# Cross-attention and gated FFN on one core: another order of the opening, and 24 idle products on TensorE

## The chip, the core and the metric

The kernel runs on one core of a Trainium2 chip. Its engines are PE (TensorE, matrix products into PSUM), DVE (VectorE), ACT (ScalarE), POOL (GpSimd) and SP (SyncE, which here only issues transfers); ACT and POOL issue some too. They run side by side and wait for each other by semaphores. The metric is the device time of one execution in microseconds (us), lower is better.

## What is computed

```python
x = x + attention(layernorm(x), ctx, ctx, pos, mask, Wq, Wk, Wv, Wo)   # rotary positions on q and k
x = x + ffn(layernorm(x), weight, bias, gate_w, in_scale, out_scale)
# x, ctx: (32, 64, 512) float32; 32 query heads, 8 key/value heads of 128
# ffn: routing = softmax(xf @ gate_w.T); (xf * (routing @ in_scale)) @ sign(weight).T * (routing @ out_scale) + bias
```

## The kernel before

The 2048 rows of x make 16 tiles of 128 rows, worked in four quarters of four tiles (512 rows). Every quarter has eight slots, one for each key/value group; slot U projects its group (K, four query heads Q1 to Q4, V), does the attention of the group before it and the output product of the group before that. So slot 0 has projections only, slot 1 projections and attention, and slot 2 is the first with output products. Slots also prepare the tiles of the next quarter (context, table rows, normalised x) and do the FFN of the quarter before; the last quarter's FFN stands at the end.

A product is kept exact to about float32 by three products of a split form: hi·hi, hi·lo, lo·hi. A projection is therefore 12 instructions on PE (four pieces of the contraction, three products each, lines 1045 to 1047) into one PSUM bank of 128x512. Each 128x512 weight tile is loaded to one of five ring buffers `raw` (SP, `load_weights`), copied by ACT to its upper half (`split_hi`, line 511), and POOL subtracts to get the lower half (`split_lo`, line 408). Three pairs of buffers hold the halves of projection weights, `w_hi` and `w_lo`; four hold those of the output weights (wo). A load waits for the split five loads before it. After a K or Q projection DVE rotates the result by the position tables (`rotate`, lines 801 and 803) and POOL adds the two parts (`rope_sum`, line 415).

The opening, ahead of slot 0, is `first_quarter` on each engine: positions go to DVE and from it to POOL, which gathers four tiles of the rotary table (line 382); four context tiles are transposed by PE (line 1034), split by ACT (hi) and DVE (lo, line 736); x's four tiles get statistics on DVE, the root on POOL (`s_rstd`, line 397), the normalisation on DVE (line 1002), and are transposed and split likewise. Then come the transposes of the table rows, whose copies on ACT are cosT and sinT. `ffn_constants` prepares the FFN: signs of its weight (DVE, lines 1015 and 1017) and their transposes, the gate's transpose, the scales. Each engine runs its instructions in the order in which they are written, so the order of the source is the schedule. STREAM is the order in which a slot's ten weight tiles (0 K, 1 to 4 Q, 5 V, 6 to 9 wo) are loaded and split.

## Time and profile before

| | us |
|---|---|
| median of 3 runs | 1192.29 |
| lowest and highest | 1191.25, 1193.23 |
| the profiled execution | 1192.27 |
| its span from first to last instruction | 1189.5 |
| PE busy | 1156.4 (97%) |
| DVE busy | 809.9 (68%) |
| POOL busy | 712.0 (60%) |
| ACT busy | 552.3 (46%) |

Busy time is the sum over an engine's instructions. A row of a timeline gives start, duration and instruction; what stands in brackets is the idle time of the engine before it and what ended that. Consecutive instructions of PE overlap, so their step (start to start) is shorter than their duration.

### The profile page before, as it was taken

How to read it: one execution, taken by the hardware profiler on the slowest of the kernel's cores; microseconds unless marked ns; L12 is line 12 of the kernel's file. 1: busy time of each engine (PE TensorE's matmuls, PEld its weight loads, DVE VectorE, ACT ScalarE, POOL GpSimd, SP SyncE). 2: the span in 40 equal slices, each digit the busy share in tenths (PEclk: the TensorE clock that was granted, in tenths of full speed). 3: DMA queues.
4: the chain of work that ended last, by engine and by line, in shares of the span. 5: the costliest groups of instructions: out<-in, count | busy, mean ns of one | idle time of the engine just before them, and what ended most of it. 6: DMA issues, size and time to landing. Idle time of an engine off the chain costs nothing.

```text
span 1189.5 us, 23750 instructions
## 1 busy us (share of the span) xinstructions
PE 1156.4 (97%) x7636; PEld 949.7 (80%) x7636; DVE 809.9 (68%) x1367; ACT 552.3 (46%) x1768; POOL 712.0 (60%) x593
## 2 busy tenths in 40 slices
PE   5699999999999999999999999999999999999997
PEld 4588888888888888888888888888888888888875
DVE  6767676667776766777766667667677666666764
ACT  3444445444543544444544544544544444535442
POOL 5666655555775656765555766655667555766525
PEclk9999999999999999999999999999999999999997
DMA  8234333223422322333322322323332222322200
GB/s 227 79 111 120 93 94 89 79 81 100 121 90 63 88 79 88 120 99 97 107 67 71 106 79 87 97 83 105 89 98 81 64 72 68 97 75 87 78 2 35
DMA packets 136923, 106.02 MB, mean 89 GB/s; under 512 B 12776, under 2 KB 111080, under 8 KB 136864
## 3 DMA queue, kind: packets, MB, share of 16 engines
q1 hardware_dynamic: 131488, 94.78, 27.5%
q10 hardware_dynamic: 4608, 8.39, 2.1%
q0 software_dynamic: 768, 2.10, 0.6%
q8 instruction: 33, 0.54, 0.2%
q14 instruction: 26, 0.21, 0.1%
HBM read 101.05 MB, written 4.19 MB: 88 GB/s over the span
## 4 chain that ended last, share of the span: by engine, by line
PE 94%; DVE 3%; POOL 1%; issue 1%; ACT 1%; DMA 0%; POOLq 0%; DVEq 0%; ACTq 0%
PE chunk L1045 25%; PE chunk L1046 24%; PE chunk L1047 24%; PE o_ps L1118 5%; PE sc_ps L1093 3%; PE tr_ps L1093 2%; PE aux L1034 2%; PE o_ps L1034 1%; PE tr_ps L1034 1%; PE sc_ps L1034 1%; PE aux L1195 1%; PE aux L1196 1%; PE aux L1169 1%; PE aux L1181 0%; ACT probs L547 0%
## 5 line engine op out<-in xcount | busy, mean ns | idle before, releaser
L408 POOL TENSOR_TENSOR w_lo<-raw,w_hi 128x512 fp32r<-128x512 f32 x192 | 247.0, 1298 | 384.6 <-ACT w_hi L511 384.4
L801 DVE TENSOR_TENSOR swp<-chunk,sinT 64x512 f32<-64x512 f32 x320 | 220.3, 689 | 98.8 <-PE chunk L1047 94.4
L1045 PE MATMUL chunk<-xT_hi,w_hi 128*128 128x512 f32 (+1 forms) x512 | 210.0, 410 | 2.0 <-POOL w_lo L408 1.8
L1046 PE MATMUL chunk<-xT_lo,w_hi 128*128 128x512 f32 (+1 forms) x512 | 201.6, 394 | 0.0
L1047 PE MATMUL chunk<-xT_hi,w_lo 128*128 128x512 f32 (+1 forms) x512 | 200.6, 392 | 0.0
L1045 PE MATMUL chunk<-wo_hi,oT_hi 128*128 128x512 f32 x496 | 196.7, 397 | 0.1
L1047 PE MATMUL chunk<-wo_hi,oT_lo 128*128 128x512 f32 x496 | 193.7, 391 | 0.0
L1046 PE MATMUL chunk<-wo_lo,oT_hi 128*128 128x512 f32 x496 | 193.2, 389 | 0.0
L415 POOL TENSOR_TENSOR qT<-qT,swp 128x512 f32<-128x512 f32 x128 | 166.1, 1298 | 41.2 <-DVE qT L803 39.2
L547 ACT ACTIVATE probs<-scores,neg_max 128x64 f32<-128x64 f32 x512 | 170.4, 335 | 28.5 <-DVE neg_max L758 28.5
L743 DVE TENSOR_TENSOR acc<-chunk,acc 128x512 f32 (+1 forms) x128 | 88.2, 689 | 139.3 <-PE chunk L1047 139.1
L408 POOL TENSOR_TENSOR wo_lo<-raw,wo_hi 128x512 fp32r<-128x512 f32 x128 | 165.1, 1302 | 0.0
L511 ACT ACTIVATE w_hi<-raw 128x512 fp32r<-128x512 f32 x192 | 117.7, 629 | 61.2 <-issue 45.9
L1045 PEld LDWEIGHTS chunk<-xT_hi,w_hi 128*128 128x128 f32 x512 | 97.2, 190 | 25.3 <-DVE qT L803 2.2
L1047 PEld LDWEIGHTS chunk<-xT_hi,w_lo 128*128 128x128 f32 x512 | 96.6, 189 | 21.8
L1046 PEld LDWEIGHTS chunk<-xT_lo,w_hi 128*128 128x128 f32 x512 | 96.8, 189 | 17.4
L1045 PEld LDWEIGHTS chunk<-wo_hi,oT_hi 128*128 128x128 f32 x496 | 93.1, 188 | 20.8 <-issue 0.5
L1047 PEld LDWEIGHTS chunk<-wo_hi,oT_lo 128*128 128x128 f32 x496 | 93.1, 188 | 20.2
L1046 PEld LDWEIGHTS chunk<-wo_lo,oT_hi 128*128 128x128 f32 x496 | 93.2, 188 | 18.0
L1045 PE MATMUL chunk<-cT_hi,w_hi 128*128 128x512 f32 (+1 forms) x256 | 99.9, 390 | 1.3 <-DVE qT L803 1.3
L511 ACT ACTIVATE oT_hi<-o_ps 128x512 fp32r<-128x512 f32 x128 | 69.5, 597 | 66.4 <-PE o_ps L1118 66.4
L1047 PE MATMUL chunk<-cT_hi,w_lo 128*128 128x512 f32 (+1 forms) x256 | 99.9, 390 | 0.0
(281 smaller groups left out, 1934.7 us busy)
## 6 DMA issues: line engine op xcount, KB each, us to landing
raw<-in_L_xattn_Wo SPq DMA_DIRECT2D x132, 256.0 KB, 2.6
raw<-in_L_xattn_Wq SPq DMA_DIRECT2D x128, 256.0 KB, 2.7
raw<-in_L_xattn_Wk SPq DMA_DIRECT2D x32, 256.0 KB
raw<-in_L_xattn_Wv SPq DMA_DIRECT2D x32, 256.0 KB
acc<-in_x ACTq DMA_DIRECT2D x16, 256.0 KB, 2.9
c_tile<-in_ctx SPq DMA_DIRECT2D x12, 256.0 KB, 3.1
x_tile<-in_x SPq DMA_DIRECT2D x12, 256.0 KB, 3.4
result<-y ACTq DMA_DIRECT2D x12, 256.0 KB, 2.1
```

The source lines that it names most:

```text
L408: nc.gpsimd.tensor_tensor(lo, raw[:, n % RING, :], hi.bitcast(F32), ALU.subtract).then_inc(wsplit_lo, 1)
L415: nc.gpsimd.tensor_tensor(dst, dst, by_batch(swp[:, j % 2, :]), ALU.add).then_inc(roped, 1)
L511: return nc.scalar.activation(dst, src, ACT.Copy)
L547: last = nc.scalar.activation(probs[:, d, bass.ts(k, S)], scores[:, 2 * d + k // 4, bass.ts(k % 4, S)], ACT.Exp, bias=neg_max[:, d, k:k + ...
L743: nc.vector.tensor_tensor(a, chunk[OUT_BANK[p]][:, :], a, ALU.add).then_inc(added, 1)
L801: last = nc.vector.tensor_tensor(swp[to, k, :], bank[of, :], sinT[to, here], ALU.mult)
L1034: return nc.tensor.transpose(dst, src, ident[:, :])
L1045: nc.tensor.matmul(bank, a_hi, b_hi, start=i == 0, stop=False)
L1046: nc.tensor.matmul(bank, a_hi, b_lo, start=False, stop=False)
L1047: last = nc.tensor.matmul(bank, a_lo, b_hi, start=False, stop=i == n - 1)
L1093: last = nc.tensor.matmul(DUO_BANK[d][a * S:(a + 1) * S, bass.ts(place, S)], qT[:, hp, queries], kT[:, bass.ts(at, S)], start=True, stop=True)
L1118: last = nc.tensor.matmul(o_both[:, b, bass.ts(i, HG * S)], v[keys, 2 * d + i, :], probs_of[keys, i, :], start=k == 0, stop=k == 2)
```

## The change

The opening is written in another order, and what belongs to it moves:

- SP no longer issues the positions; ACT does, as its first transfer, then context tiles 2 and 3 and x tiles 2 and 3. SP issues context 0 and 1, K's weight, x tiles 0 and 1, and V's, Q1's, Q2's and Q3's weights, Q4's when a buffer is free, and only then the constants.
- Slot 0 loads six weight tiles in the order K, V, Q1 to Q4 (`FIRST_STREAM`); its four wo loads and splits, of a group that slot 0 does not have, are gone. All later ring numbers shift by it.
- PE does K's projection between context's and x's transposes, and V's ahead of Q's. PE gets 8, 12 and 4 products of the identity with itself in three places of `first_quarter`, into a bank nobody reads before it is written again.
- POOL clears its four buffers ahead of the gathers, and splits K and V ahead of the root of x and Q1 behind it; in slot 0 it alternates split and sum, and it splits the next slot's first two tiles there.
- The signs of the FFN weight are taken by ACT in place in slot 0 (`ACT.Sign`), no longer by DVE in two instructions a tile. PE's constants come behind all of slot 0's projections.
- Slot 1 has an order of its own on PE, DVE and ACT (`first_attention`): K's projection ahead of the scores, three projections between the scores and the transposes of the probabilities, and two weight splits between the exponentials of the two halves.

PE in the opening, from the last context tile (o_ps<-ident,qT) on: x_tile, f_tile, fT and y are the four normalised x tiles, scores holds the table rows, cT is the transposed context. Before:

```order
L1034 MATMUL o_ps<-ident,qT 128x128 x4
L1034 MATMUL chunk<-ident,x_tile 128x128 x4
L1034 MATMUL chunk<-ident,f_tile 128x128 x4
L1034 MATMUL o_ps<-ident,fT 128x128 x4
L1034 MATMUL aux<-ident,y 128x128 x4
L1034 MATMUL sc_ps<-ident,scores 128x128 x4
L1034 MATMUL tr_ps<-ident,scores 128x128 x4
L1045 MATMUL chunk<-cT_hi,w_hi 128x512
```

And in the change:

```order
L1122 MATMUL o_ps<-ident,qT 128x128 x4
L1393 MATMUL chunk<-ident 128x128 x12
L1133 MATMUL chunk<-cT_hi,w_hi 128x512
...
L1393 MATMUL chunk<-ident 128x128 x4
L1122 MATMUL chunk<-ident,x_tile 128x128 x4
L1122 MATMUL o_ps<-ident,f_tile 128x128 x4
L1122 MATMUL sc_ps<-ident,fT 128x128 x4
L1122 MATMUL aux<-ident,y 128x128 x4
L1122 MATMUL tr_ps<-ident,scores 128x128 x4
L1122 MATMUL o_ps<-ident,scores 128x128 x4
```

K's projection has moved from behind the table rows to ahead of x, between two groups of idle products.

POOL from its constants to the first sums (w_lo is a split, kT and qT are sums). Before:

```order
L388 MEMSET half 128x4
L382 DMA scores<-rope_table,pos_first 128x256 x4
L393 MEMSET c_tile 128x512
L393 MEMSET vT 128x512
L393 MEMSET probs 128x512
L393 MEMSET route 128x128
L397 TENSOR_TENSOR s_rstd<-s_var,half 128x4
L408 TENSOR_TENSOR w_lo<-raw,w_hi 128x512 x4
L408 TENSOR_TENSOR wo_lo<-raw,wo_hi 128x512
L461 MEMSET scores 128x1024
L415 TENSOR_TENSOR kT<-kT,swp 128x512
```

And in the change:

```order
L409 MEMSET half 128x4
L411 MEMSET c_tile 128x512
L411 MEMSET probs 128x512 x2
L411 MEMSET route 128x128
L403 DMA scores<-rope_table,pos_first 128x256 x4
L422 TENSOR_TENSOR w_lo<-raw,w_hi 128x512 x2
L536 TENSOR_TENSOR s_rstd<-s_var,half 128x4
L422 TENSOR_TENSOR w_lo<-raw,w_hi 128x512
L539 MEMSET scores 128x1024
L422 TENSOR_TENSOR w_lo<-raw,w_hi 128x512
L429 TENSOR_TENSOR kT<-kT,swp 128x512
```

The memsets went ahead of the gathers, two splits went ahead of s_rstd, and the wo split is gone.

ACT in slot 1, from V's rows (v_hi) to the values' first half (oT_hi). Before:

```order
L511 ACTIVATE v_hi<-o_ps 128x512
L511 ACTIVATE w_hi<-raw 128x512
L547 ACTIVATE probs,ssum<-scores,neg_max 128x64 x16
L511 ACTIVATE pT_hi<-sc_ps 128x512
L511 ACTIVATE w_hi<-raw 128x512
L511 ACTIVATE wo_hi<-raw 128x512
L511 ACTIVATE pT_hi<-tr_ps 128x512
L511 ACTIVATE oT_hi<-o_ps 128x2x4x64 x2
```

And in the change:

```order
L548 ACTIVATE v_hi<-o_ps 128x512
L548 ACTIVATE w_hi<-raw 128x512
L584 ACTIVATE probs,ssum<-scores,neg_max 128x64 x8
L548 ACTIVATE wo_hi<-raw 128x512
L548 ACTIVATE w_hi<-raw 128x512
L584 ACTIVATE probs,ssum<-scores,neg_max 128x64 x8
L548 ACTIVATE wo_hi<-raw 128x512
L548 ACTIVATE w_hi<-raw 128x512
L548 ACTIVATE pT_hi<-sc_ps 128x512
L548 ACTIVATE pT_hi<-tr_ps 128x512
L548 ACTIVATE oT_hi<-o_ps 128x2x4x64 x2
```

The 16 exponentials are cut in two halves with two splits between them, and two splits moved ahead of the probabilities' first copy.

The diff, cut to its core:

```diff
+    FIRST_STREAM = [0, PROJ - 1, 1, 2, 3, 4]
+        def ring_use(s, n):
+            return (n % RING, n // RING + 1) if s.first_proj else ((n - HG) % RING, 2 * s.U + (n - HG) // RING + 1)
+        def split_count(s, n):
+            return n + 1 if s.first_proj else s.U * CH - HG + n + 1
...
+                    if s.first_proj and n == 0:
+                        for p in range(2):
+                            sp.dma_start(acc[:, p, :], row_of(x_t, p)).then_inc(x_first_in[p], 16)
+                if s.first_proj:
+                    load_constants()
...
 # POOL
+            def first_projections(s):
+                second = Slot(0, 1, False, False)
+                for n in range(3, PROJ):
+                    split_lo(s, n)
+                    rope_sum(s, n - 3)
+                split_lo(second, 0)
+                rope_sum(s, KQ - 2)
+                split_lo(second, 1)
+                rope_sum(s, KQ - 1)
...
+            def first_quarter():
+                wait_alone(pool, pos_first_ok, 1)
+                for p in range(PAIRS):
+                    gather_rows(rows_first[:, p, :], pos_first[:, p:p + 1]).then_inc(rows_first_in, 16)
+                split_lo(first, 0)
+                split_lo(first, 1)
+                pool.wait_ge(x_st3, PAIRS)
+                nc.gpsimd.tensor_tensor(s_rstd[:, :], s_var[:, :], half[:, :], ALU.pow).then_inc(x_st4, PAIRS)
+                split_lo(first, 2)
+                wait_alone(pool, rows_tr, PAIRS)
+                nc.gpsimd.memset(scores[:, :, :], MASKED).then_inc(fill_ok, 1)
...
 # ACT
+            def first_projections(s):
+                split_hi(s, 3)
+                v_out(s)
+                split_hi(s, 4)
+                act.wait_ge(fw_in, 16)
+                for c in range(EC):
+                    nc.scalar.activation(fw[:, c, :], fw[:, c, :], ACT.Sign).then_inc(fw_sgn, 1)
+                split_hi(s, 5)
+                act.wait_ge(sc_in, 16 * 6)
...
 # PE
+            def first_projections(s):
+                for j in (5, 1, 2, 3, 4):
+                    project(s, j)
+                ffn_constants()
+            def first_attention(s):
+                project(s, 0)
+                pe.wait_ge(gate_ok, 1)
+                pe.wait_ge(fw_ok, EC)
+                v_rows(s)
+                scores_of(s, 0)
+                scores_of(s, 1)
+                project(s, 1)
+                project(s, 2)
+                project(s, 3)
+                probs_T(s, 0)
+                probs_T(s, 1)
+                project(s, 4)
+                values(s, 0)
+                project(s, 5)
+                pe.wait_ge(sc_lo, 2)
+                values(s, 1)
...
+            def idle_products(count):
+                for n in range(count):
+                    nc.tensor.matmul(chunk[0][:, bass.ts(n % EC, P)], ident[:, :], ident[:, :], start=True, stop=True)
...
                 pe.wait_ge(ident_ok, 2)
+                idle_products(8)
                 for p in range(PAIRS):
                     pe.wait_ge(c_first_in[p], 16)
                     transpose_tile(C_BANK[p], c_first[:, p, :]).then_inc(c_tr, 1)
+                idle_products(12)
+                project(Slot(0, 0, False, False), 0)
+                idle_products(4)
                 for p in range(PAIRS):
                     pe.wait_ge(xn_ok, p + 1)
                     transpose_tile(X_BANK[p], x_first[p]).then_inc(x_tr, 1)
...
 # DVE
+            def first_attention(s):
+                v_lo_split(s)
+                soft_a(s, 0)
+                soft_a(s, 1)
+                rotate(s, 0)
+                rotate(s, 1)
+                soft_b(s, 0)
+                soft_b(s, 1)
+                rotate(s, 2)
+                pT_lo_split(s, 0)
+                rotate(s, 3)
+                pT_lo_split(s, 1)
+                out_lo(s, 0)
+                out_lo(s, 1)
+                rotate(s, 4)
+                out_lo(s, 2)
+                out_lo(s, 3)
```

## Rows read from the trace of the kernel before

**Rows 1.** Stretches: us, busy PE, PEld, DVE, ACT, POOL (instructions), clock, DMA share, GB/s.

```profile
0.00:75.29 75.29, 52.52 (x304) 42.14 (x305) 53.16 (x82) 30.83 (x80) 46.22 (x47) 0.98 0.53 146
75.29:1160.00 1084.71, 1083.27 (x7243) 890.05 (x7242) 743.76 (x1258) 513.48 (x1667) 650.20 (x534) 1.00 0.29 87
1160.00:1189.50 29.50, 20.65 (x92) 17.47 (x90) 12.96 (x28) 7.94 (x22) 15.59 (x13) 0.75 0.09 36
```

**Rows 2.** PE's waits up to 75 us: us in total, times, longest.

```profile
PE aux L1034 <- DMA qT<-in_ctx: 7.9, 1, 7.9
PE chunk L1034 <- DVE x_tile L1002: 5.4, 1, 5.4
PE tr_ps L1034 <- DVE probs L768: 2.0, 1, 2.0
PE chunk L1045 <- POOL w_lo L408: 1.8, 1, 1.8
PE sc_ps L1034 <- DVE probs L768: 1.7, 1, 1.7
```

**Rows 3.** Timeline of PE: start us, us, instructions; in brackets idle before and releaser.

```profile
17.30 1.11 PE L1034 MATMUL chunk<-ident,x_tile 128*128 128x128 f32 x4 [5.42 <-DVE x_tile L1002]
...
19.91 1.06 PE L1034 MATMUL aux<-ident,y 128*128 128x128 f32 x4
20.77 0.67 PE L1034 MATMUL sc_ps<-ident,scores 128*128 128x128 f32 x4
...
21.63 0.47 PE L1045 MATMUL chunk<-cT_hi,w_hi 128*128 128x512 f32 x1
...
24.48 0.39 PE L1045 MATMUL chunk<-xT_hi,w_hi 128*128 128x512 f32 x1
...
75.29 0.39 PE L1045 MATMUL chunk<-wo_hi,oT_hi 128*128 128x512 f32 x1
```

**Rows 4.** Busy time by stretch, around the low clock in slot 1.

```profile
58.40:62.00 3.60, 3.60 (x10) 2.66 (x9) 1.51 (x3) 0.00 (x0) 2.68 (x3) 0.53 0.53 145
```

**Rows 5.** Timeline of POOL.

```profile
10.88 0.95 POOL L382 DMA_INDIRECT scores<-rope_table,pos_first  x1 [0.30 <-issue]
...
14.67 1.06 POOL L397 TENSOR_TENSOR s_rstd<-s_var,half 128x4 f32<-128x4 f32 x1 [1.23 <-DVE s_var L999]
15.71 1.25 POOL L408 TENSOR_TENSOR w_lo<-raw,w_hi 128x512 fp32r<-128x512 f32 x1
...
38.24 1.75 POOL L408 TENSOR_TENSOR wo_lo<-raw,wo_hi 128x512 fp32r<-128x512 f32 x1
```

**Rows 6.** Timeline of DVE.

```profile
5.15 0.18 DVE L978 CAST pos_f<-pos_i 128x16 f32<-128x16 int32 x1 [5.15 <-DMA pos_i<-in_pos_BxS]
...
15.76 1.49 DVE L1002 TENSOR_SCALAR x_tile<-acc,s_mv,s_rstd 128x512 f32<-128x512 f32 x1 [1.27 <-POOL s_rstd L397]
17.17 0.54 DVE L1002 TENSOR_SCALAR f_tile<-acc,s_mv,s_rstd 128x512 f32<-128x512 f32 x1
...
22.25 1.55 DVE L1015 TENSOR_SCALAR probs<-acc 128x512 f32<-128x512 f32 x1
...
30.64 0.69 DVE L1017 SCALAR_TENSOR_TENSOR acc<-acc,probs 128x512 f32<-128x512 f32 x1
```

**Rows 7.** Timeline of PE, the router's logits in a loop slot.

```profile
364.44 0.96 PE L1169 MATMUL aux<-gateT,fT 128*128 128x8 f32 x8
```

**Rows 8.** Busy time by stretch, early transfers.

```profile
5.00:10.00 5.00, 2.02 (x9) 1.66 (x10) 1.72 (x6) 0.60 (x1) 2.47 (x3) 1.00 1.01 352
```

**Rows 9.** The page's groups: busy us, mean ns, idle before and releaser.

```profile
L408 POOL TENSOR_TENSOR w_lo<-raw,w_hi 128x512 fp32r<-128x512 f32 x192 | 247.0, 1298 | 384.6 <-ACT w_hi L511 384.4
L801 DVE TENSOR_TENSOR swp<-chunk,sinT 64x512 f32<-64x512 f32 x320 | 220.3, 689 | 98.8 <-PE chunk L1047 94.4
...
L415 POOL TENSOR_TENSOR qT<-qT,swp 128x512 f32<-128x512 f32 x128 | 166.1, 1298 | 41.2 <-DVE qT L803 39.2
```

**Rows 10.** Groups by form up to 75.29 us.

```profile
L547 ACT ACTIVATE probs<-scores,neg_max 128x64 f32<-128x64 f32 x16 | 5.3, 334 | 2.4 <-DVE neg_max L758 2.4
```

More of the change, by code:

```diff
@@ L270, in jobs_of, with loads_of, rank, proj_bank @@
             return t, f, tile_in(s, i) if s.residual else None
+        def loads_of(s):
+            return FIRST_STREAM if s.first_proj else STREAM if s.proj else [PROJ + h for h in range(HG)]
+        def ring_use(s, n):
+            return (n % RING, n // RING + 1) if s.first_proj else ((n - HG) % RING, 2 * s.U + (n - HG) // RING + 1)
+        def split_count(s, n):
+            return n + 1 if s.first_proj else s.U * CH - HG + n + 1
+        def rank(s, j):
+            return FIRST_STREAM.index(j) if s.first_proj else j
+        def proj_bank(s, j):
+            return chunk[0 if s.first_proj and j == PROJ - 1 else PROJ_BANK[j]]
         def one(tile):
@@ L320, in load_weights @@
             def load_weights(s):
-                for n in range(CH):
-                    if s.first_proj and n == RING:
-                        load_constants()
-                    c, r = STREAM[n], n % RING
+                for n, c in enumerate(loads_of(s)):
+                    r, _ = ring_use(s, n)
                     if c >= PROJ:
@@ L451, in slot @@
                 if s.proj:
-                    for n in range(3):
+                    for n in range(2 if s.first_attn else 0, 3):
                         split_lo(s, n)
@@ L458, in slot @@
                     split_lo(s, 4)
-                if s.first_proj:
-                    wait_alone(pool, rows_tr, PAIRS)
-                    nc.gpsimd.memset(scores[:, :, :], MASKED).then_inc(fill_ok, 1)
-                if s.proj:
                     rope_sum(s, 0)
@@ L516, in split_hi @@
             def split_hi(s, n):
-                c = STREAM[n] if s.proj else PROJ + n
-                r = n % RING
-                act.wait_ge(raw_in[r], 16 * ((CH // RING) * s.U + n // RING + 1))
+                c, (r, use) = loads_of(s)[n], ring_use(s, n)
+                act.wait_ge(raw_in[r], 16 * use)
                 if c < PROJ:
-                    if not (s.first_proj and c < WRING):
-                        act.wait_ge(proj_done, s.U * PROJ + c - WRING + 1)
-                    hi = flat(w_hi[:, c % WRING, :, :])
+                    k = rank(s, c)
+                    if not (s.first_proj and k < WRING):
+                        act.wait_ge(proj_done, s.U * PROJ + k - WRING + 1)
+                    hi = flat(w_hi[:, k % WRING, :, :])
                 elif s.proj:
@@ L633, in attend_last @@
                 pT_hi_split(s, 1)
+            def first_attention(s):
+                ffn_constants()
+                split_hi(s, 2)
+                v_in_rows(s)
+                split_hi(s, 3)
+                exp_duo(s, 0)
+                split_hi(s, 4)
+                split_hi(s, 5)
+                exp_duo(s, 1)
+                split_hi(s, 6)
+                split_hi(s, 7)
+                pT_hi_split(s, 0)
+                pT_hi_split(s, 1)
+                out_hi(s, 0)
+                out_hi(s, 1)
+                split_hi(s, 8)
+                split_hi(s, 9)
+                v_out(s)
+                out_hi(s, 2)
+                out_hi(s, 3)
+            def first_projections(s):
+                split_hi(s, 3)
+                v_out(s)
+                split_hi(s, 4)
+                act.wait_ge(fw_in, 16)
+                for c in range(EC):
+                    nc.scalar.activation(fw[:, c, :], fw[:, c, :], ACT.Sign).then_inc(fw_sgn, 1)
+                split_hi(s, 5)
+                act.wait_ge(sc_in, 16 * 6)
+                copy(in_sc[:, :], in_raw[:, :]).then_inc(sc_hi, 1)
+                copy(out_sc[:, :], out_raw[:, :]).then_inc(sc_hi, 1)
+                second = Slot(0, 1, False, False)
+                split_hi(second, 0)
+                split_hi(second, 1)
             def slot(s):
@@ L638, in slot @@
                     return attend_last(s)
-                if s.proj and not s.first_proj:
+                if s.first_proj:
+                    return first_projections(s)
+                if s.first_attn:
+                    return first_attention(s)
+                if s.proj:
                     split_hi(s, 0)
```

151 lines of the change are left out of this document (72 added, 79 removed).

## The prediction

> **What bounds the kernel now.** I read three views, the stretches first. The busy time by stretch [rows 1] shows where PE is short of work in the span of 1189.5 us: from 75.29 us, when slot 2 begins with the first output product, until 1160 us PE is busy 1083.27 of 1084.71 us, while the opening has 52.52 busy of 75.29 us. So the middle costs what PE's instructions cost, and an edit of the opening is worth exactly what it moves slot 2's start, if nothing new waits afterwards. The waits of PE before 75 us [rows 2] name the losses: 7.9 us for the first context tile, 5.4 us for the normalised x, then 1 to 2 us each for softmax, a weight split and a rotation. The timeline [rows 3] gives the marks: x transposes from 17.30, the first projection (K) at 21.63, the second at 24.48, slot 2 at 75.29.
>
> A projection is 12 products, 2.85 us for the first (21.63 to 24.48), 0.228 a step and 2.73 in all where they follow each other.
>
> **TensorE's clock.** Four transposes step in 0.85 us at 19.91 and in 0.50 at 20.77 [rows 3], which are the two levels of 1.2 and 2.4 GHz, although the clock column says 1.00 there; the engine had done transposes without a gap since 17.30. From 58.4 to 62.0 us the column says 0.53 [rows 4], after PE had stood for 1.7 and 2.0 us [rows 2]: half the rate for 3.4 us, a loss of 1.7. The Trainium skill, page "TensorE: Matmul & The Clock Gate", section "Part 4: PE-mode transpose", says that transposes do not engage the full clock as they do not count as busy. The trace disagrees: nothing but transposes stood between 17.30 and the step up. By the page only the idle products and K's could raise the clock, and if those came too late the first rival below would be the result, 1181.0 us; by the row the clock is up before K and the sum stands.
>
> **Part 1, until x is transposed.** Times are those of before, re-chained.
> POOL: the four gathers end at 10.88 + 0.95 = 11.83 [rows 5]. They hang on the positions, which reach DVE at 5.15 [rows 6] after an issue at 0.8 from SP; now ACT issues them first at the same moment, so I keep 11.83. The four memsets (1.9 us there) move ahead of the gathers, into time in which POOL stood: nothing. Behind the gathers stand now two splits (K, V), 1.25 each [rows 5], ending at 13.1 and 14.35, and then s_rstd, 1.06 [rows 5], until 15.5. Before, it ended at 15.73. So K ahead of x costs x nothing: s_rstd is late by its place in POOL's order, but no later than it was.
> DVE: the first norm takes 1.49 instead of 0.54 [rows 6] beside POOL's split, and will again, as a split follows s_rstd as before. x tiles are ready at 17.0, 17.5, 17.95, 18.4 (steps of 0.46).
> PE: K's products wait for K's lower half, 13.1, and run to 15.9 at the full level. The four idle products, then x's transposes at 17.05, paced by the norms, end at 18.9; eight transposes of table rows, 1.0 us (20.77 to 21.63 before, at the full level but for the first), end at 19.9. V starts at 19.95. Before, K started at 21.63 [rows 3]. **Gain: 1.7 plus K's 2.7, 4.4 us.**
> Idle products: their price is not in the trace. Logits (four f32 products, two records each) take 0.96 us [rows 7] at the full level, so 0.24 a product for 8 columns, which I take; a product of 128 columns might cost twice that. At the low level it is 0.43 (records step as transposes do) to 0.85. The first 8 stand from 1.6 us while the context is on its way: over at 5.0 to 8.4, nothing, since context is wanted only by 13.1. The 12 end by 11.5 to 13.6: nothing to 0.5. The upper end with both at the low level (8.4, 11.9, then 12 x 0.43) is 17 and costs x some 2.4 us. The last 4 (1.0) end at 16.9, before 17.05. Without a reason for a gain in themselves, I book them at nothing and their effect as the clock.
> DMA: from 5 to 10 us the queues move 352 GB/s [rows 8]. Ahead of the last x tile stand 2.25 MB (context, x, K) and up to 1.25 MB that shares the engines (V, two Q, gathers): it lands between 10 and 13.6. It has to be there by 13.1 (statistics 1.3 us, s_rstd's turn at 14.35): nothing, at worst 0.5 us.
>
> **Part 2, from 19.95 to slot 2.** PE's own work: 11 projections 30.0, constants 5 x 0.44 = 2.2, V's rows 0.5, scores 2.0, probabilities 0.9, values 1.8: 37.4 us, thus 57.4 at the soonest. Before, 12 projections and the same 7.4 took 53.7 (21.63 to 75.29), so 13.5 us were waits and low clock. What waits now, from durations of 1.30 a split and a sum, 3 x 0.69 = 2.1 a rotation [rows 9], 2.65 for eight exponentials (8 x 0.33 [rows 10]):
> The signs leave DVE, where they stood for 9.1 us (22.25 to 31.33 [rows 6]) ahead of the first rotation; ACT makes them in 4 x 0.5 us after 24, when it has nothing else. K is rotated 21.2 to 23.4, Q1 (done 25.6) to 27.8. POOL alternates split and sum: split 3 until 23.0, 4 until 26.0, 5 until 30.4. Q3 may start at 26.0 and does at 28.3; Q4 may at 30.4 and starts at 31.0. No wo load is split here now: 4 x 1.3 us less on POOL in slot 0, which it does behind. Last rotation 36.0, last sum 37.4. PE does constants and the next K in 33.8 to 38.8, V's rows to 39.3 and scores at once: PE's waits there, for a split (1.8 [rows 2]), a rotation and a sum, go.
> Slot 1: softmax's first maximum 41.8, exponentials to 44.5 and 48.2 (a split and two between), rotations 43.2 to 47.5, normalised 48.3 and 49.2. PE runs three projections meanwhile, 41.3 to 49.6: the transposes of both halves wait for nothing, where they waited 1.7 and 2.0. Q4 50.5, values 53.2, V 54.2 (third rotation 54.1: level), values 57.1 to 58.0. The output product waits for the last wo split: out_hi ends at 55.8, ACT 0.5, two splits of 1.25, 58.8. Here about 1 us is left; with small gaps in the five level places I take 2.0 in all, bounds 0.3 and 5. **Slot 2 starts at 59.4, 15.9 us sooner.** Work behind it (rotation 4, sum, wo splits) ends by 60.3, and scores there are wanted at 62.
>
> **Part 3, the loops and the end.** The same instructions in the same order, with ring numbers shifted by one and the same distance between load and split: nothing. In the last stretch the clock averages 0.75 [rows 1]; where its low part falls can shift by a few products: 1.7 us either way.
>
> **Sum.** The profiled execution took 1192.27 us, 2.8 over its span, and lies at the median of the three runs, 1192.29. 1192.3 - 4.4 - (13.5 - 2.0) = 1176.4.
>
> **Rivals.**
> Low clock in the opening: the idle products do not raise it, and K, x's and the rows' transposes go at half. For: they did until 20.77. Against: 12 idle products and K's twelve follow each other. K 13.2 to 18.3, products 20, transposes 23.5, rows 24.6: 4.6 us, 1181.0. Chance 0.08.
> POOL sets the pace: from 19.95 it has a memset and 22 pieces, 28.7 us at 1.30, against 37.4 of PE; beside DVE's two-input work pieces of 1.75 occur [rows 5], and all level places depend on it. Late weights work alike. Price 3, 1179.4. Chance 0.14.
> Softmax still waits: the splits put between ACT's exponentials hold them, and 3.7 us of waits with 1.7 of low clock stay. 5.4 us, 1181.8. Chance 0.07.
> Idle products too long, as priced above: 2.4 us, 1178.8. Chance 0.05.
> Better than the walk: no wait left and a luckier end, 1173.5. Chance 0.06.
> Little comes of it: x or its transposes come 4 us later by DMA and all 11.5 us of waits stay; 1192. Chance 0.01.
> Slower: the shifted ring makes a split late in every loop slot. In the loops PE waits for a split that POOL makes from a buffer whose load waits for the split five earlier; if that came short by a piece, 1.3 us a slot, 31 slots, 40 us: 1216. It decides from 0.5 us a slot. Against: 1.4 us idle in the whole middle [rows 1] and an unchanged distance. Chance 0.03.
>
> **How the numbers follow.** The forecast, 1174 to 1179, has 0.56. Adding POOL's and the products' cases and most of the two at 1181 to 1182 gives 1173.5 to 1181.5 for eight in ten. A measurement can tell 0.2%, 2.4 us, from no change: faster 0.95, same 0.02, slower 0.03.
>
> **What would show it.** In the profile after: V's products at 19 to 21 us, K's ended before x's transposes; s_rstd ending at 15 to 16; x's transposes stepping 0.44 a tile, not 0.87; no DVE signs; PE waits before slot 2 under 6 us behind 20 us, none over 1.5; a clock of 1.00 from 13 us to the last stretch; the first output product at 58 to 61. I am wrong if s_rstd or a weight comes later than 17, if PE stands over 2 us between projections, or if the middle has new idle.

## Result and the profile after

The changed kernel takes 1177.47 us (four runs, 1177.19 to 1177.51), the kernel before 1191.89 in the runs beside it (1191.25 to 1193.23): a ratio of 0.9877, 95% interval 0.9860 to 0.9894, or 14.4 us less. The forecast was 1176.4 us, with a range of 1173.5 to 1181.5. The profiled execution took 1177.43 us, its span 1175.6. One execution each of e5_slot1_generic, e8_root_first and e10_both and one of the kernel before took 250 to 1100 us longer than the others of its kernel and is left out of every figure below, though the 1176.68 in the expectation of e10_both still counts one.

The first view of the kernel after is the busy time by stretch, as in [rows 1] (us, busy PE, PEld, DVE, ACT, POOL with instructions, clock, DMA share, GB/s). The stretches are the opening up to slot 2, the loops, the end.

```profile
0.00:60.62 60.62, 54.67 (x352) 45.93 (x353) 44.15 (x70) 31.17 (x81) 41.70 (x42) 1.00 0.60 163
60.62:1145.00 1084.38, 1082.63 (x7238) 889.60 (x7239) 745.00 (x1260) 513.05 (x1666) 649.95 (x534) 1.00 0.29 87
1145.00:1175.60 30.60, 21.76 (x95) 18.34 (x94) 13.61 (x30) 8.10 (x22) 15.65 (x14) 0.76 0.09 35
```

The opening shrank from 75.29 to 60.62 us, and the middle is as full as before. PE's busy time in the opening rose by 2.15 us (7.67 us are idle products; the other work took 5.5 us less, a good part of which had been at the low level before); what fell is its standing time, from 22.77 to 5.95 us.

PE's waits up to slot 2 (us in total, times, longest), to be read against [rows 2]:

```profile
PE chunk L1393 <- POOL ident L407: 1.6, 1, 1.6
PE tr_ps L1122 <- DMA qT<-in_ctx: 1.5, 1, 1.5
PE chunk L1133 <- POOL w_lo L422: 1.4, 2, 0.8
PE chunk L1133 <- POOL wo_lo L422: 0.8, 1, 0.8
...
PE tr_ps L1122 <- DVE probs L843: 0.2, 1, 0.2
```

The 7.9 us for context and the 5.4 us for x are gone from the list, softmax's 2.0 and 1.7 are 0.2. No single wait is over 1.6.

PE's timeline (start us, us, instructions; in brackets the idle time before and its releaser), which answers [rows 3]. L1393 are the idle products, L1122 transposes, L1133 the first product of a step of a projection, L1206 the attention's values:

```profile
1.55 3.78 PE L1393 MATMUL chunk<-ident 128*128 128x128 f32 x16 [1.55 <-POOL ident L407]
...
9.93 2.84 PE L1393 MATMUL chunk<-ident 128*128 128x128 f32 x24
13.58 0.47 PE L1133 MATMUL chunk<-cT_hi,w_hi 128*128 128x512 f32 x1 [0.80 <-POOL w_lo L422]
...
16.42 1.05 PE L1393 MATMUL chunk<-ident 128*128 128x128 f32 x8
17.54 0.65 PE L1122 MATMUL chunk<-ident,x_tile 128*128 128x128 f32 x4
18.03 0.62 PE L1122 MATMUL o_ps<-ident,f_tile 128*128 128x128 f32 x4
...
20.20 0.48 PE L1133 MATMUL chunk<-cT_hi,w_hi 128*128 128x512 f32 x1
20.51 0.40 PE L1134 MATMUL chunk<-cT_lo,w_hi 128*128 128x512 f32 x1
...
50.56 0.66 PE L1122 MATMUL tr_ps<-ident,probs 128*128 128x128 f32 x4 [0.23 <-DVE probs L843]
51.78 0.47 PE L1133 MATMUL chunk<-xT_hi,w_hi 128*128 128x512 f32 x1 [0.56 <-POOL w_lo L422]
...
58.83 0.39 PE L1206 MATMUL o_ps<-pT_hi,v_hi 64*128 64x256 f32 x2 [0.16 <-DVE oT_lo L811]
...
60.62 0.49 PE L1133 MATMUL chunk<-wo_hi,oT_hi 128*128 128x512 f32 x1 [0.83 <-POOL wo_lo L422]
```

K's projection stands at 13.58, ahead of x's transposes (17.54); V's starts at 20.20, and slot 2 at 60.62, 14.67 us sooner than at 75.29. x's transposes step by 0.46 to 0.49, not 0.87: the clock is at 2.4 GHz by then.

POOL's timeline answers [rows 5]:

```profile
11.18 0.95 POOL L403 DMA_INDIRECT scores<-rope_table,pos_first  x1 [0.30 <-issue]
12.14 2.53 POOL L422 TENSOR_TENSOR w_lo<-raw,w_hi 128x512 fp32r<-128x512 f32 x2
14.89 1.06 POOL L536 TENSOR_TENSOR s_rstd<-s_var,half 128x4 f32<-128x4 f32 x1 [0.21 <-DVE s_var L1099]
15.93 1.27 POOL L422 TENSOR_TENSOR w_lo<-raw,w_hi 128x512 fp32r<-128x512 f32 x1
...
57.95 2.52 POOL L422 TENSOR_TENSOR wo_lo<-raw,wo_hi 128x512 fp32r<-128x512 f32 x2 [1.12 <-ACT wo_hi L548]
```

s_rstd comes behind two splits and still ends at 15.95, against 15.73 before. The last fence's final row is the wait of 0.83 in PE's list: POOL itself had waited 1.12 us for ScalarE's high part of the out_proj weights.

**Where the 13.9 us of span went.** Up to V's first product: K was started at 21.63 and took 2.85 there, V now starts at 20.20, so 1.43 + 2.85 = 4.28 us. From there to slot 2: 75.29 - 24.48 = 50.81 before, 60.62 - 20.20 = 40.42 now, 10.39 us. Behind slot 2: 1189.5 - 75.29 = 1114.21 before, 1114.98 now, 0.77 us the other way. 4.28 + 10.39 - 0.77 = 13.9.

### The profile page after: what moved, and what is told of

It reads as the page before. It is cut to its first block, busy times and chain, and to the rows that moved or that the text cites. A ratio compares the mean times of both kernels' runs of the same rounds, so it can differ in the third digit from the quotient of the medians.

```text
span 1175.6 us, 23824 instructions
## 1 busy us (share of the span) xinstructions
PE 1159.1 (99%) x7684; PEld 953.9 (81%) x7684; DVE 802.8 (68%) x1359; ACT 552.3 (47%) x1768; POOL 707.3 (60%) x589
## 4 chain that ended last, share of the span: by engine, by line
PE 95%; DVE 1%; POOL 1%; ACT 1%; issue 1%; DMA 1%; POOLq 0%; ACTq 0%; DVEq 0%
PE chunk L1133 25%; PE chunk L1134 24%; PE chunk L1135 24%; PE o_ps L1206 5%; PE sc_ps L1181 3%; PE tr_ps L1181 2%; PE aux L1122 2%; PE o_ps L1122 2%; PE tr_ps L1122 1%; PE sc_ps L1122 1%; PE aux L1286 1%; PE aux L1287 1%; PE aux L1260 1%; DMA qT<-in_ctx 1%; PE aux L1272 0%
## 5 line engine op out<-in xcount | busy, mean ns | idle before, releaser
L1133 PE MATMUL chunk<-xT_hi,w_hi 128*128 128x512 f32 (+1 forms) x512 | 208.9, 408 | 0.6 <-POOL w_lo L422 0.6
L1133 PE MATMUL chunk<-wo_hi,oT_hi 128*128 128x512 f32 x496 | 196.8, 397 | 1.2 <-POOL wo_lo L422 0.8
L422 POOL TENSOR_TENSOR wo_lo<-raw,wo_hi 128x512 fp32r<-128x512 f32 x124 | 159.3, 1297 | 4.8 <-ACT wo_hi L548 4.8
L1133 PEld LDWEIGHTS chunk<-xT_hi,w_hi 128*128 128x128 f32 x512 | 96.9, 189 | 23.2 <-issue 0.8
L1133 PEld LDWEIGHTS chunk<-wo_hi,oT_hi 128*128 128x128 f32 x496 | 93.1, 188 | 22.1 <-issue 1.8
L1133 PE MATMUL chunk<-cT_hi,w_hi 128*128 128x512 f32 (+1 forms) x256 | 100.0, 391 | 0.8 <-POOL w_lo L422 0.8
L1134 PE MATMUL chunk<-cT_lo,w_hi 128*128 128x512 f32 (+1 forms) x256 | 99.8, 390 | 0.0
```

Source lines behind the costliest of these rows:

```text
L422: nc.gpsimd.tensor_tensor(lo, raw[:, r, :], hi.bitcast(F32), ALU.subtract).then_inc(wsplit_lo, 1)
L1133: nc.tensor.matmul(bank, a_hi, b_hi, start=i == 0, stop=False)
L1134: nc.tensor.matmul(bank, a_hi, b_lo, start=False, stop=False)
```

## The experiments

All marks come from one profiled execution of each kernel (us): K's, x's transposes', V's and slot 2's first instruction on PE, the distance from V to slot 2, the span behind slot 2, and that execution's time. "Times" are the lowest and highest of the kernel's runs. The runs came in several batches, in which the kernel before had medians of 1191.7 to 1192.3 us.

| kernel | K | x | V | slot 2 | V to slot 2 | rest | run | times |
|---|---|---|---|---|---|---|---|---|
| after | 13.58 | 17.54 | 20.20 | 60.62 | 40.42 | 1114.98 | 1177.43 | 1177.19 to 1177.51 |
| e12_after_again | 13.47 | 17.43 | 20.09 | 60.50 | 40.41 | 1114.90 | 1177.25 | 1177.12 to 1177.82 |
| e1_no_idle | 13.65 | 18.91 | 21.66 | 62.05 | 40.39 | 1115.15 | 1178.99 | 1177.19 to 1179.27 |
| e2_no_idle12 | 13.67 | 17.94 | 20.48 | 60.88 | 40.40 | 1114.42 | 1177.82 | 1177.82 to 1178.95 |
| e3_k_behind_x | 20.35 | 17.69 | 23.19 | 63.44 | 40.25 | 1115.56 | 1180.83 | 1179.99 to 1181.71 |
| e4_signs_dve | 14.38 | 18.11 | 20.65 | 67.23 | 46.58 | 1114.97 | 1184.01 | 1181.66 to 1184.01 |
| e5_slot1_generic | 13.95 | 17.68 | 20.23 | 67.44 | 47.21 | 1113.86 | 1183.17 | 1183.17 to 1184.77 |
| e6_exps_together | 14.12 | 17.84 | 20.38 | 64.72 | 44.34 | 1115.78 | 1182.35 | 1180.84 to 1182.59 |
| e8_root_first | 14.37 | 17.23 | 19.77 | 60.15 | 40.38 | 1114.55 | 1176.49 | 1175.98 to 1176.87 |
| e9_wo_early | 14.38 | 18.11 | 20.65 | 60.15 | 39.50 | 1114.95 | 1176.90 | 1176.39 to 1177.88 |
| e10_both | 13.78 | 16.60 | 19.14 | 58.62 | 39.48 | 1114.88 | 1175.29 | 1174.90 to 1175.57 |
| e11_consts_early | 14.13 | 17.87 | 20.41 | 60.76 | 40.35 | 1114.54 | 1177.12 | 1176.45 to 1178.00 |

The loops are the same in all of them, and their "rest" lies between 1113.86 and 1115.78. So an effect of under about 1 us has to be read from the marks, and from V to slot 2 above all, since V's own place also moves with the clock in the opening (below); the last column by itself does not settle it. The eight runs of the changed kernel in the first two rows have a median of 1177.39, which the differences below are taken against.

### The ruler: the changed kernel again

> The changed kernel itself once more, unedited, beside the three others on the same chip, as the ruler for differences of under 1 us: 1177.4 us, 0.3 either way. Where the opening's low clock falls otherwise than in its first profile (idle products or K's products at half the level), V's first product comes up to 0.8 us from 20.20 and the time moves with it.

1177.30 us (1177.12 to 1177.82), ratio 0.9879 (0.9862 to 0.9895). V came 0.11 us sooner and slot 2 0.12 sooner than in the first profile: the marks repeat to about 0.1 us.

### Without the idle products

```
-                idle_products(8)
...
-                idle_products(12)
...
-                idle_products(4)
```

> The change without its 24 idle products; all else as it stands. Theory of order (the gain is the moved work, the products only lift PE's clock a little sooner): K's projection begins at the low clock and is raised on its way, x's transposes start 1 to 1.5 us later than 17.5, V's products 0.7 to 3 us later than 20.2, so 1178 to 1180.5 us, likeliest 1179. Theory of the clock (the products carry a large part): the clock stays low until 20 us or more and the time rises by 4.6 us or more, over 1182.

1178.68 us (0.9887, 0.9870 to 0.9903), 1.3 us more. PE's timeline of e1_no_idle, K and what follows:

```profile
13.65 0.77 PE L1133 MATMUL chunk<-cT_hi,w_hi 128*128 128x512 f32 x1 [2.85 <-POOL w_lo L422]
14.21 0.63 PE L1134 MATMUL chunk<-cT_lo,w_hi 128*128 128x512 f32 x1
...
18.48 0.63 PE L1135 MATMUL chunk<-cT_hi,w_lo 128*128 128x512 f32 x1
18.91 0.81 PE L1122 MATMUL chunk<-ident,x_tile 128*128 128x128 f32 x4
19.56 0.60 PE L1122 MATMUL o_ps<-ident,f_tile 128*128 128x128 f32 x4
```

K starts at the same place but its products step by 0.43 instead of 0.23, the 1.2 GHz level, for all twelve; it holds x's transposes until 18.91, and V comes 1.46 us later. The level rises with x's transposes, so nothing behind them is slower. That is what the idle products buy: the level of K's projection, 1.3 us of the 14.4. One of the four runs, at 1177.19 us, was no slower than the changed kernel; it has no trace. The new order alone keeps 1191.7 - 1178.7 = 13.0, against the kernel before in the runs beside it.

With the first eight kept and only the twelve and the four out:

> Only the first 8 idle products stay, the 12 ahead of K and the 4 behind it are out. If the clock, once up at 7.3 us, outlives PE's idle time up to K's products (some 3.7 us with one product group missing), K and x are unchanged and the time is 1177.4 within 0.3 (the last 4 even stood in x's way by at most 0.2). If it falls there, K's 12 products or x's transposes go at half rate and it is 1178.5 to 1180.

1178.31 us (0.9889, 0.9872 to 0.9905), 0.9 us more. Here K's first seven products ran at the low level (steps of 0.43 until 16.79) and the others at the full one, so V came 0.28 us later than in the first profile; the profiled execution was the fastest of the four. The stretch at the low level in e2_no_idle12:

```profile
10.00:16.80 6.80, 3.38 (x10) 2.49 (x9) 5.42 (x11) 1.86 (x3) 6.24 (x6) 0.50 1.05 286
```

PE's wait of 3.42 us for K's split began only at 10.25, so it is not the wait that lost the level here. In the eight edited forms of the changed kernel that keep the twelve, the traces have a low stretch there too. It begins between 8.4 and 10.6 and is over between 11.8 and 14.0, over transposes and idle products, and every K behind it ran at the full level. The two traces of the changed kernel itself show no such stretch. So the eight in front do not keep the level up, and with the twelve directly ahead of K the level is back when K starts. The twelve without the eight were not run.

### The idle products alone, in the kernel before

```
+                idle_products(8)
                 for p in range(PAIRS):
                     pe.wait_ge(c_first_in[p], 16)
                     transpose_tile(C_BANK[p], c_first[:, p, :]).then_inc(c_tr, 1)
+                idle_products(12)
+                idle_products(4)
```

> The kernel before with 8 idle products ahead of the context's transposes and 16 behind them, nothing else changed: the products alone. Theory of order: x's transposes go at 0.46 a tile instead of 0.85, K starts at 20.1 instead of 21.6, but the signs on DVE wait for their weight (landed at 22) and hold the first rotation, so slot 2 moves by 0 to 1.5 us: 1190.5 to 1192.3. Theory of the clock: 4 us or more are gained, under 1188.

1191.07 us against 1192.32, ratio 0.9989 (0.9979 to 0.9999), 1.3 us less. PE's timeline of e7_before_plus_idle:

```profile
11.78 4.98 PE L1280 MATMUL chunk<-ident 128*128 128x128 f32 x32
17.42 0.66 PE L1034 MATMUL chunk<-ident,x_tile 128*128 128x128 f32 x4 [0.66 <-DVE x_tile L1002]
17.92 0.61 PE L1034 MATMUL chunk<-ident,f_tile 128*128 128x128 f32 x4
...
20.07 0.48 PE L1045 MATMUL chunk<-cT_hi,w_hi 128*128 128x512 f32 x1
```

x's transposes now step by 0.44 to 0.50 where they had stepped by 0.87, and K starts at 20.07 instead of 21.63. Slot 2 came 1.63 us sooner (73.66), although this execution had a low stretch more than the kernel before, from 38.2 to 41.8; PE's wait of 1.29 us at 42.73 in the kernel before is gone in return. So the products act by the clock, in either kernel, and are worth about 1.3 us.

### K behind x again

```
-                project(Slot(0, 0, False, False), 0)
...
                     transpose(bank[:, bass.ts(2 + i, P)], rows_first[:, p, P:2 * P]).then_inc(rows_tr, 1)
+                project(Slot(0, 0, False, False), 0)
```

> K's projection stands again behind the table rows on PE, everything else of the change stays. Theory of order: its 2.7 us leave the time in which PE waited for x, so V and all behind it start 2.7 us later less what POOL's and DVE's waits behind absorb: 1179.5 to 1180.2, likeliest 1180.0. Rival: POOL and DVE set slot 0's pace and not PE; then it is 1177.4 to 1178.2.

1180.52 us (0.9906, 0.9890 to 0.9923), 3.1 us more. PE waits 2.19 us for x_tile and starts x's transposes at 17.69, as with K in front (17.54). K runs behind them and V starts at 23.19, 2.99 us later. K ahead of x is thus worth its length, and costs x nothing. PE's timeline of e3_k_behind_x:

```profile
17.69 0.66 PE L1122 MATMUL chunk<-ident,x_tile 128*128 128x128 f32 x4 [2.19 <-DVE x_tile L1102]
...
20.35 0.48 PE L1133 MATMUL chunk<-cT_hi,w_hi 128*128 128x512 f32 x1
```

### Part 2: the signs on VectorE again

```
-                act.wait_ge(fw_in, 16)
-                for c in range(EC):
-                    nc.scalar.activation(fw[:, c, :], fw[:, c, :], ACT.Sign).then_inc(fw_sgn, 1)
...
+                if s.first_proj:
+                    signs()
                 if s.proj:
                     rotate(s, 0)
```

> The signs of the FFN weight are taken by DVE in two instructions a tile ahead of the first rotation, as before, and not by ACT. Theory of order: the first rotation moves from 21.5 to 29 or 30 us (8 instructions of 0.5 to 1.8 us), the second Q projection behind the first waits for it and PE stands 2 to 5 us in slot 0: 1180 to 1183, likeliest 1181.5. Rival (the signs were covered, the gain came from elsewhere): under 1178.5.

1183.23 us (0.9924, 0.9907 to 0.9940), 5.8 us more and just above the expected 1180 to 1183 us. VectorE makes the signs from 21.78 to 27.55, so K is rotated at 27.58 instead of 21.50. POOL adds K's rotated halves before it splits the next weights, and PE stands for that split. PE's wait in the timeline of e4_signs_dve, and the stretch (columns as above) around it:

```profile
32.48 0.77 PE L1143 MATMUL chunk<-xT_hi,w_hi 128*128 128x512 f32 x1 [3.42 <-POOL w_lo L423]
```

```profile
30.90:37.90 7.00, 5.42 (x13) 4.33 (x14) 2.98 (x5) 0.00 (x0) 6.38 (x6) 0.51 0.28 75
```

The wait is 3.42 us. The granted clock fell at 31.0, while PE still stood, and was low until 37.8: twelve products at steps of 0.43 instead of 0.23. V to slot 2 is 6.16 us longer, of which the wait is 3.4 and the low clock 2.5.

### Part 2: slot 1 in the order of the loop slots

```
                 if s.first_attn:
-                    return first_attention(s)
+                    pe.wait_ge(gate_ok, 1)
+                    pe.wait_ge(fw_ok, EC)
+                    pe.wait_ge(sc_lo, 2)
```

(and on VectorE and ScalarE the slot's own order is left out in the same way)

> Slot 1 runs in the order of the other slots on PE, DVE and ACT, as in the kernel before; the rest of the change stays. Theory of order: only one projection stands between the scores and the transposes of the probabilities, so PE waits again 3 to 4 us for softmax, perhaps followed by some 1.7 us of low clock: 1181 to 1184, likeliest 1182.5. Rival: the waits of slot 1 came from what slot 0 left late (POOL and the rotations), and with slot 0 in order they are gone in any order: 1177.4 to 1179.

1183.88 us (0.9931, 0.9909 to 0.9952), 6.5 us more. PE's waits up to slot 2 of e5_slot1_generic:

```profile
PE o_ps L1120 <- DVE out_sc L811: 2.6, 1, 2.6
PE tr_ps L1120 <- DVE probs L843: 2.0, 1, 2.0
...
PE sc_ps L1120 <- DVE probs L843: 0.8, 1, 0.8
```

and its granted clock, two of the stretches:

```profile
36.00:44.00 8.00, 5.39 (x75) 4.76 (x74) 5.65 (x8) 3.25 (x12) 3.18 (x3) 0.79 0.19 62
...
48.00:52.00 4.00, 2.60 (x10) 2.11 (x11) 3.47 (x6) 1.91 (x6) 2.53 (x3) 0.76 0.05 16
```

The kernel's V starts at 20.23, as after, and slot 2 comes 6.82 us later. PE waits for softmax again, 0.75 and 1.99 us where [rows 2] has 1.7 and 2.0, so the rival (slot 0 in order makes them go in any order of slot 1) is out; after the 1.99 the projection steps by 0.43 until 53.54. The wait of 2.61 us is one that this experiment needs itself (the slot's first transposes go into banks that the constants use), with a low stretch of its own, so not all of the 6.8 is the price of the order: softmax's share is 2.7 us of waits and about 1.6 of low clock.

### Part 2: the sixteen exponentials together

```
                 exp_duo(s, 0)
+                exp_duo(s, 1)
                 split_hi(s, 4)
                 split_hi(s, 5)
-                exp_duo(s, 1)
                 split_hi(s, 6)
```

> In slot 1 ACT does all 16 exponentials together and only then the two splits that stood between them. Theory: POOL gets its wo split 2.6 us later (48.3 for 45.7), the sums and the split that Q4's projection waits for come that much later, PE's wait of 0.6 there grows to 2 to 3: 1179 to 1180. Rival: softmax bounds the slot, the second half comes 1.1 us earlier, and the time stays or falls: 1176.8 to 1177.6.

1181.82 us (0.9908, 0.9890 to 0.9925), 4.4 us more, where 1179 to 1180 us was expected. The mechanism held and its size did not. PE's wait in e6_exps_together, and the stretch behind it:

```profile
54.35 0.76 PE L1133 MATMUL chunk<-xT_hi,w_hi 128*128 128x512 f32 x1 [3.00 <-POOL w_lo L422]
```

```profile
54.50:58.00 3.50, 3.50 (x9) 2.76 (x10) 2.15 (x4) 0.00 (x0) 3.50 (x4) 0.55 0.51 151
```

The wait of 0.56 for the split of Q4's weight became 3.00, 2.4 us, and the level was low for 3.4 us from its end on, another 1.5. The probabilities came no sooner: their first transposes started at 49.87, and the second waited the same 0.23. So putting two splits between the exponentials is what POOL's row needs, and the prediction's third rival (the splits hold the exponentials, softmax still waits) fails: the second half of the probabilities is ready within 0.23 us of PE.

### Improving it: s_rstd straight behind K's split

```
                 split_lo(first, 0)
-                split_lo(first, 1)
                 pool.wait_ge(consts, 1)
                 pool.wait_ge(x_st3, PAIRS)
                 nc.gpsimd.tensor_tensor(s_rstd[:, :], s_var[:, :], half[:, :], ALU.pow).then_inc(x_st4, PAIRS)
+                pool.wait_ge(xn_ok, PAIRS)
+                split_lo(first, 1)
                 split_lo(first, 2)
...
-                idle_products(4)
```

> POOL does the root of x directly behind K's split and splits V and Q1 only behind the four norms; the last 4 idle products are out. Theory: s_rstd ends at 14.7 instead of 15.95, the first norm takes 0.5 instead of 1.5, x's transposes start right behind K's products at 16.4 instead of 17.5, V's products at 19.1 to 19.3 instead of 20.2, and slot 2 comes 0.9 to 1.1 us sooner: 1176.4. Rival: V's or Q1's split, now ending at 18 and 19.2, or POOL's clearing of scores behind them is late next and takes it back: 1177.2 to 1178.

1176.49 us (0.9864, 0.9843 to 0.9886), 0.9 us less, with all three runs below all eight of the changed kernel. VectorE's timeline of the changed kernel, where splits of POOL run at 12.14 to 14.67 and from 15.93:

```profile
13.29 1.42 DVE L1099 TENSOR_SCALAR s_var<-s_mv 128x4 f32<-128x4 f32 x1
15.98 1.50 DVE L1102 TENSOR_SCALAR x_tile<-acc,s_mv,s_rstd 128x512 f32<-128x512 f32 x1 [1.27 <-POOL s_rstd L536]
```

and that of e8_root_first, where none runs beside either:

```profile
13.64 0.17 DVE L1100 TENSOR_SCALAR s_var<-s_mv 128x4 f32<-128x4 f32 x1
15.08 0.55 DVE L1103 TENSOR_SCALAR x_tile<-acc,s_mv,s_rstd 128x512 f32<-128x512 f32 x1 [1.27 <-POOL s_rstd L535]
```

The same two instructions take 0.17 instead of 1.42 and 0.55 instead of 1.50 us. x is normalised 1.85 us sooner (15.63 against 17.48), but in this run the twelve idle products took 4.12 us, being partly at the low level, and K did not start before 14.37; so x's transposes waited for PE and V came only 0.43 us sooner. The four idle products behind K, 1.05 us in the changed kernel, would have held x's transposes by as much again; the two parts of the edit were not tried apart.

### Improving it: out_proj's weights earlier on ScalarE

```
                 pT_hi_split(s, 0)
+                split_hi(s, 8)
+                split_hi(s, 9)
                 pT_hi_split(s, 1)
                 out_hi(s, 0)
                 out_hi(s, 1)
-                split_hi(s, 8)
-                split_hi(s, 9)
                 v_out(s)
```

> The changed kernel with one move: in slot 1 ScalarE makes the high parts of out_proj's two weight tiles (splits 8 and 9) ahead of pT_hi(1) and out_hi, not behind them. Theory that PE's wait of 0.83 us at the first out_proj product (60.62 us) is that of a chain (ScalarE wo_hi 57.23, GpSimd split 57.95, PE): the wait goes, the first out_proj product comes at 59.8, and the time is 0.7 to 0.9 us shorter, 1176.6 us. Rival, that the pT_hi(1) thus made 0.6 to 0.8 us later is what PE waits for next: a wait of 0.3 to 0.8 us at the second half of the values, and the time as that of the changed kernel, 1177.4 us.

1176.70 us (0.9875, 0.9858 to 0.9891), 0.7 us less; one of its four runs, 1177.88, is as slow as the slowest of the changed kernel, so the time alone would not settle it. The marks do: V to slot 2 is 39.50 instead of 40.42 and 40.41. POOL's splits in e9_wo_early start without a wait, 0.76 us sooner although V was 0.45 later:

```profile
55.94 1.29 POOL L429 TENSOR_TENSOR qT<-qT,swp 128x512 f32<-128x512 f32 x1 [0.15 <-DVE qT L878]
57.19 2.54 POOL L422 TENSOR_TENSOR wo_lo<-raw,wo_hi 128x512 fp32r<-128x512 f32 x2
```

PE's wait of 0.83 is gone, and the one before the second half of the values stayed at 0.16, so the rival (a later pT_hi is waited for) is out. Slot 2 came 0.47 sooner than after, since this run's opening was 0.45 later by the clock: its twelve idle products took 4.47 us against 2.84.

### Both

> The GpSimd order of the earlier run (s_rstd straight behind K's split, V's and Q1's splits behind the norms, the last four idle products out) together with the early out_proj weights. Theory that the two chains are far apart (16 us and 58 us) and both on PE's path: their gains add, 0.8 (1176.68 against 1177.47) and 0.8, to 1175.9 us. Rival, that a gain at the opening is taken back by a wait in slot 1 (where PE would reach the probabilities sooner than they are made): 1176.6 us.

1175.29 us (0.9860, 0.9841 to 0.9880), 2.1 us less than the changed kernel and the fastest of all that ran; its slowest run is 1.55 us under the changed kernel's fastest. The two add up, and to more than the 1175.9 that was expected: V at 19.14 (1.06 sooner) and V to slot 2 at 39.48 (0.94 less). The 1.06 is more than in the run before because the twelve idle products took 3.47 here and K could start at 13.78. Its x transposes follow K without a gap, in PE's timeline of e10_both:

```profile
16.38 0.39 PE L1136 MATMUL chunk<-cT_hi,w_lo 128*128 128x512 f32 x1
16.60 0.60 PE L1123 MATMUL chunk<-ident,x_tile 128*128 128x128 f32 x4
```

### The constants' transfers early again

```
                 for n, c in enumerate(loads_of(s)):
+                    if s.first_proj and n == RING:
+                        load_constants()
...
-                if s.first_proj:
-                    load_constants()
```

> The changed kernel with the constants' transfers (ffn_w, mask, gate, scales, bias) issued ahead of Q4's weights, as before, not behind them. Theory that the constants' place does nothing for PE in this kernel, since the weights have slack: within 0.3 us of the changed kernel, 1177.4 us, the sign functions of ScalarE some 1 us sooner. Rival, that the transfers (0.5 MB) delay the weights of Q2 to Q4 or of slot 1 so that PE waits for them: 1178.5 us or more, with a wait of 1 us on a weight tile's DMA.

1177.39 us (0.9878, 0.9862 to 0.9895): the same. V to slot 2 is 40.35. "Constants late" does nothing for the time of this kernel.

## Why the prediction was right, point by point

The forecast was 1.1 us under the time. By its own steps:

- **Part 1, K ahead of x and x's own chain.** Right. The sum had s_rstd's end at 15.5, x's transposes at 17.05 and V at 19.95; they came at 15.95, 17.54 and 20.20. The e3_k_behind_x run confirms the reason: x starts no sooner without K in front. s_rstd was 0.45 late: 0.3 is the positions, which I had kept at 5.15 and which reached VectorE at 5.46, so that the gathers ended at 12.13 instead of 11.83, and the rest lies in the 0.21 that POOL then waited for s_var. From x's transposes to V it took 2.66 instead of 2.90, which gave 0.24 back. "K ahead of x costs x nothing" is right against the kernel before. But the e8_root_first run shows what the sum had taken as given: that the norm "takes 1.49 again, as a split follows". It was avoidable.
- **The idle products.** Right in both halves: a product of 128 columns took 0.45 us at the low level (eight from 1.55 to 5.12) and 2.84 / 12 = 0.24 at the full one, about the values taken (0.43 and 0.24), not the doubled ends of the range. "Nothing by themselves, and their effect as the clock" is what e1_no_idle and e7_before_plus_idle show, 1.3 us each. The rival that they are too long happened in part: in all seven other kernels with the twelve ahead of K they were partly at the low level (3.47 to 4.47 us) and K started at 13.78 to 14.38 instead of 13.58. Their lateness lies within the 2.4 us that the prediction gave as the upper end, and the sum had it at nothing. That the changed kernel's own two traces have them at the full level is a piece of luck: none of those seven edits touches what PE does before K.
- **The clock rival** (products do not raise it): false, K ran at steps of 0.23 from its first product. For the rule of the Trainium skill that was weighed there ("TensorE: Matmul & The Clock Gate", Part 4, transposes do not raise the level), [rows 3] had shown the opposite, and no run here added to that.
- **Part 2.** The waits were sized right: 2.0 us taken, and measured 0.23 + 0.56 + 0.16 + 0.83 = 1.78. The last of them is the out_proj weight of which the prediction said "about 1 us is left", and 0.83 it was; its split ended at 60.47 where the walk had 58.8, but it hangs on the first values, for which ScalarE waited and which PE had reached 1.5 us late itself. **The term that was mis-sized is PE's own work**, 37.4 us in the sum and 60.62 - 20.20 - 1.78 = 38.64 measured:

| piece | in the sum | measured |
|---|---|---|
| 11 projections | 30.0 | 30.88 |
| constants | 2.2 | 2.10 |
| V's rows | 0.5 | 0.53 |
| scores | 2.0 | 2.01 |
| probabilities | 0.9 | 1.26 |
| values | 1.8 | 1.86 |

A projection is 2.73 only among its like. PE's first step behind another kind of work takes 0.30 to 0.34 instead of 0.228 (20.20 to 20.51 above), at five places, and in front of a wait the last instruction's whole length counts: a row in brackets says how long PE stood, and another 0.16 (0.39 - 0.23) is lost beside it while its last instruction ends. The same prices had been taken for the kernel before, and there they turned PE's own time into waits: the prediction books 13.5 us of waits and low clock behind 21.63, and the trace of before has eight waits of 9.4 us together and 1.6 of low clock, 11.0.

- **POOL sets the pace** (the rival at 1179.4): it did not, but the mechanism is there. POOL's pieces beside VectorE's work of two inputs took 1.7 us where the sum had 1.30. POOL's timeline of the changed kernel, and VectorE's in the same stretches:

```profile
36.40 1.73 POOL L429 TENSOR_TENSOR qT<-qT,swp 128x512 f32<-128x512 f32 x1 [0.21 <-DVE qT L878]
38.08 1.73 POOL L422 TENSOR_TENSOR w_lo<-raw,w_hi 128x512 fp32r<-128x512 f32 x1
...
48.21 1.75 POOL L429 TENSOR_TENSOR qT<-qT,swp 128x512 f32<-128x512 f32 x1
49.92 1.71 POOL L422 TENSOR_TENSOR w_lo<-raw,w_hi 128x512 fp32r<-128x512 f32 x1
```

```profile
36.89 1.77 DVE L811 TENSOR_TENSOR out_sc<-probs,out_sc 32x512 fp32r<-32x512 f32 x1
...
49.07 1.43 DVE L843 TENSOR_TENSOR probs<-probs,srec 128x512 f32<-128x512 f32 x1
```

Each of these VectorE instructions has both inputs in SBUF. The rotations read one input from PSUM and take 0.69 a piece, with POOL at 1.27 to 1.29 beside them. The two late pieces at 48.21 and 49.92 (0.9 us over 1.28 twice) are what the wait of 0.56 at 51.78 consists of, by their place in POOL's row. That was not tried by itself.

The Trainium skill, page "SBUF — State Buffer", section "Who interferes with whom", says that a VectorE instruction with two inputs in SBUF contends with a GpSimd instruction that reads SBUF, and that one with at most one SBUF input outside the two-port modes does not. The trace agrees, with the 1.73 and 1.77 us above against 1.29 and 0.69. The same section counts tensor_scalar among those that can enter a two-port mode, which fits x's norm at 1.50 beside a split and 0.55 without one.

- **Part 3.** Right: the distance from slot 2 to the end is 1114.98 against 1114.21, within the 1.7 us either way that was given, and within the 1113.86 to 1115.78 of the kernels that share these loops. What lies outside the span was 1.8 us instead of 2.8. That these two nearly cancel is luck.

Together: slot 2 at 60.62 against 59.4 (+1.2), the rest +0.8, outside the span -0.9: +1.1 us.

What is known of the 14.4 us by experiment: the idle products 1.3, K ahead of x 3.1. The rest is Part 2, where the signs (6.2 by the marks), the exponentials' order (3.9) and slot 1's order as a whole (up to 6.8, with a wait of the experiment's own) each cost a large part when undone. They do not add to the 10.4 us between V and slot 2, since the waits overlap and one low stretch may stand for two causes. How much each had cost in the kernel before stays open. Not tried by themselves were the four splits of wo weights that slot 0 no longer has, POOL's alternation of split and sum, V ahead of Q, and the positions on ScalarE's queue.

## What to carry to other kernels

Price a wait of PE with what comes behind it. Behind V's start, or K's in the kernel before, the waits of 1.99 to 3.42 us (six in five kernels) all came with a stretch at half the clock that cost another 1.3 to 2.5 us, and those up to 1.3 us with none; an expected 2 us became 4.4 in part by that. The length alone does not tell: of two waits for the same split, 1.83 us in the kernel before was followed by none and 1.87 in e7_before_plus_idle by one (38.2 to 41.8), and the 2.19 us ahead of x in e3_k_behind_x by none. The filling pays directly ahead of the work whose level matters, not early. And look at what runs beside a short instruction on a chain: two small VectorE steps here took 2.2 us more than they need, and moving two splits of POOL behind them, with the out_proj weights earlier on ScalarE, made the kernel 2.1 us faster than the change as given.

## What the runs showed of the hardware that I had not expected

- A VectorE instruction on 128x4 elements, 0.17 us by itself, took 1.42 us while POOL had a 128x512 split at work: it ended at 14.71, with POOL's split at 14.67. A norm of 128x512 took 1.50 instead of 0.55.
- The level falls for unlike lengths: with the wait of 3.42 us the granted clock was low for some 6.8 us, the first 1.5 of them before the wait was over, and with 3.00 us and 1.99 us for 3.4. And it is not at the same place in every execution: the same twelve idle products took between 2.84 and 4.47 us in kernels in which PE has the same instructions up to there.
- The clock column shows 1.00 at the very start of a trace, while transposes of four step by 0.86 us (5.12 to 5.98), twice their full-level 0.44; there the steps have to be read, not the column. In e1_no_idle it shows 1.00 even from 13.65 to 18.91, over K's whole projection at steps of 0.43.
